# Selective-scan kernel: VectorE runs two scans, the next even drive, then the product; GpSimd finishes delta

## What is computed

```python
delta = softplus(dt_r @ W_delta + b_delta)
# per position t, per channel d and state n:
dA = exp(dt[:, :, None] * A)
h = dA * h + (dt * u_t)[:, :, None] * B_t[:, None, :]
y = einsum('bdn,bn->bd', h, C_t) + Dv * u_t
```

## Time and profile before

| | |
|---|---|
| time, median of 3 runs | 22490.82 us (22447.25 to 22503.7) |
| the profiled execution | 22505.68 us |
| its span, first to last instruction | 22503.9 us |
| mean granted TensorE clock | 0.894 |
| 62 loop iterations | about 345 us each |

### The profile page before, as it was taken

One profiled execution on the slowest core, in us unless ns is written; L12 is line 12 of the kernel. 1 busy time (PEld: TensorE's weight loads), 2 busy tenths in 40 slices (PEclk: granted clock), 3 DMA queues, 4 the chain that ended last, 5 costly groups with the idle time before them and its releaser, 6 DMA issues.

```text
span 22503.9 us, 334261 instructions
## 1 busy us (share of the span) xinstructions
PE 18818.0 (84%) x100834; PEld 6890.1 (31%) x100834; DVE 19251.1 (86%) x17938; ACT 15624.5 (69%) x21098; POOL 6356.1 (28%) x3909
## 2 busy tenths in 40 slices
PE   5888888888888888888888888888888888888887
PEld 1333333333333333333333333333333333333332
DVE  4888888888888888888888888888888888888887
ACT  3767777777677677776776777767767767777674
POOL 1222222222222222222222222222222222222222
PEclk8889898898898998988988889889889898898898
DMA  5555555555555555555555555545555555555552
GB/s 144 143 135 140 140 138 139 135 144 137 132 142 138 137 142 135 143 138 134 140 141 133 140 136 141 140 133 143 138 133 143 139 139 141 134 142 136 134 141 75
DMA packets 1418366, 3083.16 MB, mean 137 GB/s; under 512 B 207812, under 2 KB 786696, under 8 KB 1407859
## 3 DMA queue, kind: packets, MB, share of 16 engines
q1 hardware_dynamic: 1372146, 2992.85, 51.6%
q10 hardware_dynamic: 44032, 64.26, 1.1%
HBM read 2796.25 MB, written 221.51 MB: 134 GB/s over the span
## 4 chain that ended last, share of the span: by engine, by line
issue 67%; POOL 15%; PE 8%; DVE 5%; ACT 4%; DMA 1%; POOLq 0%; ACTq 0%; SPq 0%; DVEq 0%
POOL drive L1576 13%; PE bank L575 3%; DVE state L1381 3%; PE state_sum L575 2%; PE pair L575 2%; POOL taps L1563 2%; ACT work L920 1%; DVE drive L1237 1%; PE scan_sum L575 1%; ACT L920 0%; ACT decay_even L920 0%; DVE work L1237 0%; ACT du L920 0%; DVE prod L1237 0%; ACT decay L920 0%
## 5 line engine op out<-in xcount | busy, mean ns | idle before, releaser
L1576 POOL TENSOR_TENSOR drive<-du,Bb 128x784 f32<-128x784 f32 x3072 | 5689.7, 1852 | 15638.6 <-DVE drive L1237 15638.6
L575 PE MATMUL state_sum<-state,fold 128*64 128x392 f32 x24576 | 5610.5, 585 | 1052.4 <-DVE state L1381 1029.9
L1381 DVE TENSOR_TENSOR_SCAN state<-decay_even,drive 128x784 f32<-128x784 f32 x3072 | 5500.2, 1790 | 128.4 <-ACT decay_even L920 17.6
L1381 DVE TENSOR_TENSOR_SCAN state<-decay,drive 128x784 f32<-128x784 f32 x3072 | 5473.3, 1782 | 0.2 <-POOL drive L1576 0.2
L920 ACT ACTIVATE decay_even<-delta,alog 128x784 f32<-128x784 f32 x3072 | 2821.6, 918 | 3240.8 <-DVE state L1381 3224.0
L1237 DVE TENSOR_TENSOR prod<-state_sum,Cb 128x784 f32<-128x784 f32 x3072 | 2950.6, 960 | 1906.4 <-PE state_sum L575 1902.4
L575 PE MATMUL scan_sum<-prod,fold 128*64 128x392 f32 x12288 | 2990.4, 568 | 1500.0 <-DVE prod L1237 1493.9
L575 PEld LDWEIGHTS state_sum<-state,fold 128*64 128x64 f32 x24576 | 1706.4, 154 | 4427.8 <-issue 2288.4
L575 PE MATMUL bank<-rep,taps 120*32 120x392 f32 x30720 | 2973.9, 514 | 96.1 <-ACT image L920 33.8
L920 ACT ACTIVATE decay<-delta,alog 128x784 f32<-128x784 f32 x3072 | 2890.3, 941 | 115.6 <-issue 72.7
L1237 DVE TENSOR_TENSOR drive<-du,Bb 128x784 f32<-128x784 f32 x3072 | 2943.0, 958 | 18.9 <-DVE work L1237 11.9
(11 more groups left out here) (169 smaller groups left out, 17504.8 us busy)
## 6 DMA issues: line engine op xcount, KB each, us to landing
Bb<-bc_rows SPq DMA_DIRECT2D x3072, 392.0 KB, 4.4
rep<-expanded_images SPq DMA_DIRECT2D x3840, 168.0 KB
Cb<-bc_rows SPq DMA_DIRECT2D x3072, 196.0 KB, 3.6
expanded_images<-image SPq DMA_DIRECT2D x1152, 112.0 KB, 2.5
rep<-conv_in_images SPq DMA_DIRECT2D x1152, 112.0 KB, 3.9
dwo<-in_pww SPq DMA_DIRECT2D x65, 1152.0 KB, 7.3
conv_in_images<-image SPq DMA_DIRECT2D x384, 112.0 KB, 3.2
xc<-xc ACTq DMA_DIRECT2D x384, 98.0 KB, 2.6
```

Source lines behind the costliest of these rows:

```text
L575: return pe.matmul(out, lhsT, rhs, start=start, stop=stop)
L1381: v.tensor_tensor_scan(state[:, j % STATES, :], DP[:, 0:L] if j % 2 == 0 else decay[:, j // 2 % DECAYS, :], drive[:, j % 2, :], 0.0, ALU.m ...
L1576: pool.tensor_tensor(drive[:, j % 2, :], du[:, 2 * s + r, :], Bb[:, b % BSLOTS, :], ALU.mult).then_inc(drive_r.sem, 1)
```

## The change

VectorE's order in a pair becomes: even scan, odd scan, the even drive of the next pair, `prod` of the pair before. Placed pieces go after the even scan and after `prod`. The even drive of the next image's first pair is made at the end of the loop's body, and the first two decays of the next image likewise. TensorE folds first and then adds the product of the pair before. There are four state buffers instead of three. ScalarE makes the odd decay of a pair ahead of the even one.

`steps` moves from VectorE to GpSimd, placed by `LOG_AT` as before. The power of the group norm moves from GpSimd to ScalarE, as a logarithm and an exponential, with the shift as a third activation. The add of `seb2` moves from VectorE into TensorE's accumulation. The places of the lead and of the tail are set anew: convolutions, far deltas, the mix of the experts, post, norms, mixer and attention move by up to some pairs.

The diff, cut to what the text speaks of (the places of the tail shift in the same manner):

```diff
-STATES = 3
+STATES = 4
...
-LEAD_LINKS = 5
+LEAD_LINKS = 4
...
-CONVS = (("expand", 0), ("expand", 1), ("expand", 2), ("conv", 0, 0), ("conv", 0, 1), ("expand", 3), ("conv", 1, 0), ("expand", 4), ("conv", 1, 1),
-         ("expand", 5), ("conv", 2, 0), ("expand", 6), ("conv", 2, 1), ("conv", 3, 0), ("expand", 7), ("conv", 3, 1), ("expand", 8),
+CONVS = (("expand", 0), ("expand", 1), ("expand", 2), ("expand", 3), ("conv", 0, 0), ("conv", 0, 1), ("conv", 1, 0), ("expand", 4), ("conv", 1, 1),
+         ("conv", 2, 0), ("expand", 5), ("conv", 2, 1), ("expand", 6), ("conv", 3, 0), ("expand", 7), ("conv", 3, 1), ("expand", 8),
          ("conv", 4, 0), ("conv", 4, 1), ("conv", 5, 0), ("conv", 5, 1))
-CONV_SLOTS = (1, 2, 3, 5, 7, 8, 9, 10, 11, 12, 13, 14, 15, 17, 18, 19, 20, 21, 23, 24, 26)
+CONV_SLOTS = (1, 2, 3, 4, 6, 7, 9, 10, 11, 13, 14, 15, 16, 17, 18, 19, 20, 21, 23, 24, 26)
 HEAD = {name: slot(k) for name, k in zip(CONVS, CONV_SLOTS)}
-HEAD.update({("hidden",): 53.1, ("gate",): 54.3, ("point", 0): 57.1, ("point", 1): 60.3, ("group",): 63.1,
-             ("proj", 0): 67.1, ("proj", 1): 68.3, ("proj", 2): 69.1, ("conv3", 0): 73.1, ("conv3", 1): 75.1, ("conv3", 2): 77.1,
-             ("mix", 0): 79.1, ("mix", 1): 80.3, ("dbl",): 81.1,
-             ("delta", 0, 0): 84.3, ("delta", 0, 1): 85.1, ("delta", 1, 0): 86.3, ("delta", 1, 1): 87.1})
-FAR = {("delta", m, h): slot(k) + SECOND * h for m, k in ((2, 4), (3, 6), (4, 16), (5, 22)) for h in range(2)}
+HEAD.update({("hidden",): 53.1, ("gate",): 55.1, ("point", 0): 58.1, ("point", 1): 60.3, ("group",): 63.1,
+             ("proj", 0): 67.1, ("proj", 1): 69.1, ("proj", 2): 71.1, ("conv3", 0): 73.1, ("conv3", 1): 75.1, ("conv3", 2): 77.1,
+             ("dbl",): 81.1, ("delta", 0, 0): 84.3, ("delta", 0, 1): 85.1, ("delta", 1, 0): 87.1, ("delta", 1, 1): 89.1,
+             ("mix", 0): 91.1, ("mix", 1): 93.1})
+FAR = {("delta", m, h): slot(k) + SECOND * h for m, k in ((2, 8), (3, 12), (4, 22), (5, 25)) for h in range(2)}
 AT = {**HEAD, **FAR}
-READ_AT = {name: at + 1.8 for name, at in HEAD.items()}
-READ_AT.update({("hidden",): 54.5, ("proj", 0): 68.5, ("proj", 1): 69.0, ("proj", 2): 70.5, ("mix", 0): 80.5, ("mix", 1): 81.0, ("dbl",): 84.5,
-                ("delta", 0, 0): 85.0, ("delta", 0, 1): 86.5, ("delta", 1, 0): 87.0, ("delta", 1, 1): 88.5})
+READ_AT = {name: at + (2.4 if name[0] in ("conv", "conv3", "mix") else 1.8) for name, at in HEAD.items()}
+READ_AT.update({("hidden",): 54.5, ("gate",): 56.5, ("dbl",): 83.9, ("delta", 0, 0): 86.0, ("delta", 0, 1): 87.0, ("delta", 1, 0): 89.0, ("delta", 1, 1): 91.0})
 READ_AT.update({("delta", m, h): AT["delta", m, 0] + (1.4, 1.8)[h] for m in range(NEAR, NK) for h in range(2)})
-LOG_AT = {0: (88.6, 90.5, 91.0), 1: (88.7, 90.6, 93.0)}
+LOG_AT = {0: (87.6, 88.6, 91.0), 1: (91.6, 92.6, 94.0)}
 LOG_AT.update({m: (AT["delta", m, 0] + 3.4, AT["delta", m, 0] + 5.4, AT["delta", m, 0] + 6.9) for m in range(NEAR, NK)})
 KERNEL_AT = ((3, 5), (7, 9), (17, 19), (25, 27), (33, 35), (41, 43))
...
+        def decay_of(j):
+
+            return decay[:, j // 2 % DECAYS, :] if j % 2 else DP[:, 0:L]
...
-                    yield 4 * q - 3.4 if q > 1 else 0.9
+                    yield 4 * q - 2.4 if q > 1 else 2.0
...
             def scan(i, *between):
                 for p in range(NP):
-                    if p >= 1:
-                        summation(i, p - 1)
-                    elif later(i):
-                        summation(i - 1, NP - 1)
-                    go_on(between, 2 * p + 1)
                     pe.wait_ge(state_r.sem, state_r.at(i, 2 * p + 2))
                     if p >= 1 or later(i):
                         pe.wait_ge(prod_r.sem, prod_r.at(i, p))
...
                             last = mm(S[64 * e:64 * e + 64, 512 * h:512 * h + HALF], fold[:, :], half(state[:, j % STATES, :], h))
                     last.then_inc(folded.sem, 1)
                     go_on(between, 2 * p + 2)
+                    if p >= 1:
+                        summation(i, p - 1)
+                    elif later(i):
+                        summation(i - 1, NP - 1)
+                    go_on(between, 2 * p + 3)
...
-                yield 2
+                yield 2.1
+                pe.wait_ge(xs_r.sem, xs_r.at(i))
+                gate(i, 0)
+                yield 2.6
                 pe.wait_ge(y_r.sem, y_r.at(i))
                 over_channels(T[0], (yk[:, 0, :], yk[:, 1, :], y[:, 2, :])).then_inc(m1_mm.sem, 1)
-                pe.wait_ge(xs_r.sem, xs_r.at(i))
-                gate(i, 0)
-                yield 4
+                yield 5
...
-                yield at + 1
+                yield at + 2
...
-                ac(zse[:, :], P[0:RHID, 0:1], ACT.Silu, bias=seb1[:, :], scale=1.0 / L).then_inc(bank_read.sem, 1)
-                yield 56.5
-                act.wait_ge(bank_read.sem, bank(span, "gate"))
-                ac(sc[:, :], scp[:, :], ACT.Sigmoid).then_inc(sc_r.sem, 1)
+                ac(zse[32:32 + RHID, :], P[32:32 + RHID, 0:1], ACT.Silu, bias=seb1[32:32 + RHID, :], scale=1.0 / L).then_inc(bank_read.sem, 1)
+                yield READ_AT["gate",]
+                act.wait_ge(bank_filled.sem, bank(span, "gate"))
+                ac(sc[:, :], P[:, 0:T0], ACT.Sigmoid).then_inc(bank_read.sem, 1)
...
+                exponentials()
+                act.wait_ge(g_var.sem, g_var.at(i))
+                ac(gst[:, 6:7], gst[:, 6:7], ACT.Ln, bias=eps[0:C, 1:2]).then_inc(g_log.sem, 1)
+                act.wait_ge(g_log.sem, g_log.at(i))
+                ac(gst[:, 6:7], gst[:, 6:7], ACT.Exp, scale=-0.5).then_inc(g_rs.sem, 1)
+                act.wait_ge(g_rs.sem, g_rs.at(i))
+                ac(gst[:, 7:8], gst[:, 7:8], ACT.Copy, scale=gst[:, 6:7]).then_inc(g_sh.sem, 1)
...
-            def scan(i, *between):
-                def decaying(j, out, back, signal):
-                    s, m, r = PAIRS[j // 2]
-                    k, n = 2 * s + r, 2 * m + j % 2
-                    exponentials()
-                    if n == 0:
-                        act.wait_ge(dl_r.sem, dl_r.at(i, k + 1))
-                    if j >= back or later(i):
-                        act.wait_ge(state_r.sem, state_r.at(i, j - back + 1))
-                    ac(out, delta[:, k, :], ACT.Exp, scale=alog[:, k, n:n + 1]).then_inc(signal.sem, 1)
-
-                def odd(j):
-                    decaying(j, decay[:, j // 2 % DECAYS, :], 2 * DECAYS, odd_r)
-
-                for j in range(0, NU, 2):
-                    decaying(j, DP[:, 0:L], 2, even_r)
-                    go_on(between, j - 1.5)
-                    odd(j + 1)
-                    go_on(between, j - 1)
+            def decaying(i, j):
+                s, m, r = PAIRS[j // 2]
+                k, n = 2 * s + r, 2 * m + j % 2
+                exponentials()
+                if m == 0:
+                    act.wait_ge(dl_r.sem, dl_r.at(i, k + 1))
+                back, signal = (2 * DECAYS, odd_r) if j % 2 else (2, even_r)
+                if j >= back or later(i):
+                    act.wait_ge(state_r.sem, state_r.at(i, j - back + 1))
+                ac(decay_of(j), delta[:, k, :], ACT.Exp, scale=alog[:, k, n:n + 1]).then_inc(signal.sem, 1)
+
+            def scan(i, ahead, *between):
+                for j in range(2, NU + 2 if ahead else NU, 2):
+                    for n in (j + 1, j):
+                        if n < NU:
+                            decaying(i, n)
+                        else:
+                            decaying(i + 1, n - NU)
+                        go_on(between, j - 2 if n > j else j - 1)
...
+            decaying(0, 0)
+            decaying(0, 1)
+            scan(0, True, *far(0, (LOOP, 0)), *ahead(1, (LOOP, 0)), Beside(stacks(2, (LOOP, 0))))
...
-                yield 55
-                v.wait_ge(bank_filled.sem, bank(span, "gate"))
-                tt(scp[:, :], P[:, 0:T0], seb2[:, :], ALU.add).then_inc(bank_read.sem, 1)
-                yield 57
-                v.wait_ge(sc_r.sem, sc_r.at(i))
+                yield 58
+                v.wait_ge(bank_read.sem, bank(span, "gate"))
...
             def pre(i, span):
-                yield 64
-                v.tensor_copy(gk[:, :], gst[:, 6:8])
+                yield 65
+                if later(i):
+                    v.wait_ge(g_sh.sem, g_sh.at(i, 0))
+                v.tensor_copy(gk[:, :], gst[:, 6:8]).then_inc(gk_r.sem, 1)
                 v.wait_ge(bank_filled.sem, bank(span, "group"))
                 v.tensor_copy(gst[:, 2:4], P[0:C, 0:2]).then_inc(bank_read.sem, 1)
                 v.wait_ge(bank_read.sem, bank(span, "group"))
                 link(tt(gst[:, 6:7], gst[:, 2:3], gst[:, 2:3], ALU.mult))
-                link(tt(gst[:, 6:7], gst[:, 3:4], gst[:, 6:7], ALU.subtract))
-                v.tensor_scalar(gst[:, 6:7], gst[:, 6:7], 1e-5, None, ALU.add).then_inc(g_rs.sem, 1)
-                yield 65
-                v.wait_ge(g_pw.sem, g_pw.at(i))
```

(49 more changed lines are left out.)

107 lines of the change are left out of this document (54 added, 53 removed).

## The result

The changed kernel takes 23346.35 us (median of 4 runs, 23301.46 to 23386.05) beside 22477.33 for the kernel before on the same chip: ratio 1.0386, 95% interval 1.0361 to 1.0412, some 870 us more where 1370 less were forecast. The profiled execution took 23324.11 us, its span 23320.8.

A forecast was written before the change was run, and what follows sets the result against it. VectorE (86%) and TensorE (84%) were taken to wait for each other by turns. Per image 25 + 162 + 136 = 323 us for 345, times 62, plus 15, saved: 21120 us; 8-in-10 range 20200 to 22050.

The forecast's parts named there:

- the 900 us named as a sign: Sign on VectorE: the wait before `prod` falls from 1902 to under 900 us, that before `scan_sum` to near nothing.
- the third sign: Sign that TensorE is late next: it is over 90% busy in the middle stretch.
- the middle stretch: Pairs 4 to 27 of an image's 48 pairs of scans: 175 us before, forecast 162, bounds 150 and 172.
- the 1852 named: Sign on GpSimd: a mean for `delta` and `du` above 1852 ns means they are held off by odd scans.
- 3 x 2.7 + 5.4 + 3.8 = 17.3: VectorE's collisions with GpSimd per image: three steps mid-image at 2.7 us, two at the end (5.4), four other operations (3.8).
- The 2.7: Collision cost to VectorE of one step moved to GpSimd: 2.2 to 3.0 us, taken as 2.7.
- 155.5 plus a third of the 19.5 us that TensorE idles there today: Forecast for pairs 4 to 27: TensorE's work plus part of its idle time, taken as 162 us for 175.
- The last stretch: Pairs 28 to 47 of an image: 145 us before, forecast 120.1 + 5.4 + 3.8 + 7 = 136, bounds 122 and 143.
- the rival that I gave 0.04: The wait moves from `prod` to the scans at the same size; time within 0.3% of 22490 us; chance 0.04.
- VectorE's 152.3: VectorE's work in pairs 4 to 27, 144.2 + 3 x 2.7 us, said to be hidden under TensorE's 155.5.
- Waits for ScalarE: ScalarE's 50 us per image before even decays cover its new activations; waiting for its logarithm put at nothing, at most 1 us a step.
- The slower rival: The odd drive sticks behind a step on GpSimd, 7.4 us a step, nothing hidden: about 23150 us; chance 0.09.

The follow-up runs named there:

- e4: The changed kernel with GpSimd's odd drives and steps computing only 16 of 784 columns from the second image on: 22405.68 us, ratio 0.9952.
- e13: e11 with TensorE's 5x5 convolution matmuls over 56 of 392 columns from the second image on: 21438.83 us, ratio 0.9544.
- e14: e11 with relu in place of Silu and sigmoid on ScalarE, so all but 66 table loads fall away: 21668.48 us, ratio 0.9632.
- e10: The changed kernel with the three z gates placed right behind an image's Silu on ScalarE: 23004.33 us, ratio 1.0223.
- e12: The changed kernel with only GpSimd's steps on 16 of 784 columns from the second image on, its odd drives whole: ratio 1.0107.
- e11: The changed kernel with the edits of e4 and e10 together: 22159.25 us, ratio 0.9848.
- e16: The kernel before, its order untouched, with relu in place of Silu and sigmoid on ScalarE, so without table loads: 22007.7 us, ratio 0.9788.

## Why the prediction was wrong

**Sizes that held.** The wait before `prod` fell below the 900 us named as a sign, `scan_sum` waits 0.5 us, and 11.7 us per image left VectorE; the third sign, TensorE over 90% busy in the middle stretch, did not come (89%). GpSimd's `delta` and `du` took 1866 and 2017 ns in the mean, above the 1852 named. Collisions came, at GpSimd's operations and at odd scans, and their sum in VectorE's own time, 15.7 us per image (e4), is close to the forecast's 3 x 2.7 + 5.4 + 3.8 = 17.3. That is partly luck. The 2.7 was put together from waits, while the 15.7 are longer operations alone; a third of them is casts, which I didn't count, and the steps have 5.8 us, where I had given them 13.5.

**The step that failed: where the stall goes.** For the middle stretch the prediction said that TensorE is late next and took "155.5 plus a third of the 19.5 us that TensorE idles there today". TensorE's work came out (157.3 in the mean), but not a third of the idle time stayed but all of it: 20.2 us. Per image VectorE's wait before `prod` in that stretch fell from 20.9 to 8.9 us, 12.0 less; in its place came 5.6 more before scans and 12 more before the tail's operations that wait for `pair` and for ScalarE (5.6 of them before the products with `rd`, which hardly waited before). e4 shows that this idle time isn't GpSimd's doing: VectorE idles 28.1 us there with GpSimd's operations short. e13 and e14 show two engines behind it, each worth some 10 us once GpSimd's operations are short and the gates joined: TensorE, at 89%, and ScalarE with its table loads. The last stretch failed in the same way: I let 7 us of waiting stay, and 23.7 did. The 8.3 us before `prod` went to nearly nothing, but 10.0 before scans came instead (0.9 before), and the tail's operations wait 12.6 where I let 5 stay (9.5 before). That is the mechanism of the rival that I gave 0.04 (the wait moves, at the same size), in both stretches, though not its time.

**A second step: collisions hidden behind TensorE.** The prediction hid 8.1 us of collisions in the middle stretch, since VectorE's 152.3 stayed under TensorE's 155.5. They were not hidden: with GpSimd's operations short (e4) VectorE has 5.8 us less to do there, its idle time stays, and the stretch is 6.1 us shorter. Whether those 6.1 us went through VectorE alone is open. TensorE's work there fell as well, 156.58 us to 150.78 for the same 973 matmuls in the images shown, with a granted clock of 0.90 in one and 0.95 in the other, and no run holds the clock fixed.

Two smaller slips: the upper bound of 172 for the middle stretch is 171 by its own rule (175 less half of 7.8), and the "half" of TensorE's idle time that waits for VectorE is two thirds by the earlier trace rows (2524 of 3686 us).

**The step put at nothing.** "Waits for ScalarE" were covered, I said, by 50 us of its idle time per image. Cover in the mean is not cover at the place: six more table loads per image, between decays at pairs 3 to 6, cost 1.6 points, some 360 us (e10). I had read what the moved pieces wait for, and not what they do to ScalarE's tables; the diff moved the gates away from the lead's Silus, and I had let the places of the tail go together as one edit.

**The slower rival** had its mechanism right for one place, and its count wrong. I wrote 7.4 us for each of six steps; one place in each image cost 6.9 us, at the others the odd drive was not late, as the argument against the rival said. That 6.9 is near 7.4 is luck: 2.8 of it stay with every operation short (e4), most of that the wait for the logarithm, which I had bounded at 1 us a step. Steps cost 627 us (e12) and with the drives 976 (e4): with the idle time that didn't shrink, that was enough to end at 23346, close to the rival's 23150, but not by its way alone.

**What stays open.** In the last stretch neither GpSimd, ScalarE's loads nor TensorE's convolutions account for the 21 to 28 us that VectorE idles in the new order. About half of the waits there are for `pair`, in the tail's chains through TensorE and ScalarE; other places for those chains were not tried. How the middle would go with both of e13's and e14's edits wasn't tried either. Nor were the other parts of the change taken one by one: the fourth state buffer, the product added behind the fold, the group norm on ScalarE and the new places of the lead; what each of them is worth isn't shown.

## What to carry to other kernels

In a kernel whose two busiest engines are both near 85%, a wait between them need not go away with its cause; here it came back elsewhere in full. Add up each engine's idle time by stretch, and unless an edit takes work from the engine that is late next, allow for most of it to come back at another place. When work is placed anew, write down for each moved piece which operation of another engine now runs beside it (a cast beside a GpSimd operation, a Silu alone between exponentials), since that can cost more than the piece (1.0 us more for a cast of 0.35, two loads of 1.28 for a Silu of 0.59). And a short chain moved to an in-order engine costs its wait plus its length to everything queued behind it: look for the one place where its input comes last.

## What the runs showed of the hardware

- A cast of 128x392 from 16-bit floats to the 8-bit format on VectorE takes 347 ns in the mean (e4), and took 1.34 us when it began beside GpSimd's 1.84 us product (the changed kernel): it ended after GpSimd did. `prod`, with one input in PSUM, runs beside the same drives at 965 ns in the mean, and at 967 with short ones (e4).
- An odd scan that began 0.03 us after GpSimd's product of 1.85 took 3.46 us instead of 1.78. In the same image two others began 0.77 and 1.40 us after such a product and took 2.75 and 2.11 (pairs 15 and 28). All three ended 1.64 us after the product did, whenever they had begun: a scan of two SBUF tiles is held until GpSimd is done, not only slowed.
- A table load takes 1283 ns in the mean of every kernel here, and in the rows above the next activation began 0.01 us behind it; all of them together are 20.5% of the changed kernel's span (2430.0 + 2353.0 of 23320.8 us), and without them both orders gain 2.1 points (e14 beside e11, e16 beside the kernel before).
- With the convolutions' matmuls short (e13) TensorE's granted clock was 0.88 in the middle stretch shown, where e11 had 0.95; TensorE was busy 127.35 of 160.81 us there. The matmuls of the fold, which had not been touched, took 583 ns in the mean of e13 and 563 in e11.
